# Attention scores from two float32r parts in 64-row halves of TensorE, in place of three bfloat16 parts in 96 rows

## The reference

```python
x = x + attention(layernorm(x), ctx)      # 16 heads of 16 columns
x = x + ffn(layernorm(x))                 # every operand rounded to FP4 in blocks of 16
# attention
Q, K, V = heads(x @ Wq), heads(ctx @ Wk), heads(ctx @ Wv)
attn = softmax(Q @ K.T * 16 ** -0.5)      # over all 1601 context rows
out  = heads_back(attn @ V) @ Wo + bo
# ffn
h = silu(fp4(x) @ fp4(w_gate).T) * (fp4(x) @ fp4(w_up).T)
y = fp4(h) @ fp4(w_down).T                # 704 hidden columns
```

## Time and profile before

| what | us |
|---|---|
| median of 3 runs | 3928.88 |
| fastest and slowest of them | 3926.39, 3929.58 |
| span of the profiled execution, first to last instruction | 3925.2 |
| the median less that span | 3.7 |
| TensorE (PE) busy | 3745.4 |
| VectorE (DVE) busy | 2997.8 |
| ScalarE (ACT) busy | 2260.4 |
| GpSimd (POOL) busy | 870.2 |

### The profile page before, as it was taken

One profiled execution on the slowest core, in us unless ns is written; L12 is line 12 of the kernel. 1 busy time (PEld: TensorE's weight loads), 2 busy tenths in 40 slices (PEclk: granted clock), 3 DMA queues, 4 the chain that ended last, 5 costly groups with the idle time before them and its releaser, 6 DMA issues.

```text
span 3925.2 us, 73982 instructions
## 1 busy us (share of the span) xinstructions
PE 3745.4 (95%) x19654; PEld 1618.5 (41%) x19654; DVE 2997.8 (76%) x6641; ACT 2260.4 (58%) x4414; POOL 870.2 (22%) x917
## 2 busy tenths in 40 slices
PE   7999999999999999999999999999999999999997
PEld 2324444344443444434444344443434434344434
DVE  6787787787877877777877777877788777878774
ACT  2656565555655556555565556656565565655562
POOL 2221212222112211222212122221222111222113
PEclk8999999999999999999999999999999999999998
DMA  2222121121211122121121211212111211211100
GB/s 64 50 48 54 22 57 34 33 51 34 50 33 42 39 42 49 26 48 36 39 55 23 53 34 34 53 34 47 36 39 41 43 46 29 45 38 39 37 22 7
DMA packets 148169, 157.83 MB, mean 40 GB/s; under 512 B 58129, under 2 KB 118818, under 8 KB 147746
## 3 DMA queue, kind: packets, MB, share of 16 engines
q1 hardware_dynamic: 147746, 152.78, 17.8%
HBM read 39.53 MB, written 8.39 MB: 12 GB/s over the span
## 4 chain that ended last, share of the span: by engine, by line
PE 78%; DVE 11%; issue 4%; ACT 4%; SPq 1%; DMA 1%; DVEq 0%; POOL 0%; ACTq 0%
PE out_ps L815 17%; PE score_ps L804 16%; PE piece_ps L829 16%; PE work L769 8%; PE work L780 5%; DVE piece_max L1096 4%; PE work L744 3%; ACT probs L913 3%; PE work L737 3%; PE work L743 2%; PE work L735 2%; PE work L722 1%; PE work L759 1%; PE work L753 1%; PE work L727 1%
## 5 line engine op out<-in xcount | busy, mean ns | idle before, releaser
L1096 DVE TENSOR_REDUCE piece_max<-piece_ps 128x1 f32<-128x400 f32 (+1 forms) x4096 | 2144.8, 568 | 680.1 <-PE piece_ps L829 665.2
L913 ACT ACTIVATE probs<-score_ps 128x512 f32<-128x512 f32 (+1 forms) x3328 | 1876.8, 597 | 1085.1 <-PE score_ps L804 1061.0
L829 PE MATMUL piece_ps<-k_stack,q_stack 96*128 96x400 bf16 (+1 forms) x4096 | 1294.0, 339 | 55.5 <-DVE piece_max L1096 51.1
L804 PE MATMUL score_ps<-q_stack,k_stack 99*128 99x512 bf16 (+1 forms) x3328 | 1269.1, 388 | 67.6 <-issue 20.9
L815 PE MATMUL out_ps<-probs,v_ones 128*17 128x512 f32 x6656 | 886.9, 605 | 2.1 <-ACT probs L913 0.9
L804 PEld LDWEIGHTS score_ps<-q_stack,k_stack 99*128 99x128 bf16 (+1 forms) x3328 | 326.1, 99 | 910.1 <-ACT probs L913 639.0
L829 PEld LDWEIGHTS piece_ps<-k_stack,q_stack 96*128 96x128 bf16 x4096 | 389.7, 98 | 700.5 <-DVE piece_max L1096 484.4
L1148 POOL TENSOR_TENSOR h<-h,h_grid 128x704 f32<-128x704 f32 (+1 forms) x68 | 111.2, 1636 | 1106.5 <-DVE h_grid L965 1106.5
L769 PE MATMUL work<-wgu_T,xq_T 128*128 128x256 f32 (+1 forms) x1440 | 345.8, 362 | 0.4 <-ACT xq_T L887 0.4
L769 PEld LDWEIGHTS work<-wgu_T,xq_T 128*128 128x128 f32 x1440 | 258.7, 189 | 49.0 <-ACT xq_T L887 3.4
L815 PEld LDWEIGHTS out_ps<-probs,v_ones 128*17 128x17 f32 x6656 | 110.6, 95 | 277.5 <-issue 233.3
(11 more groups left out here) (142 smaller groups left out, 2846.0 us busy)
## 6 DMA issues: line engine op xcount, KB each, us to landing
k_stack<-k_parts SPq DMA_DIRECT2D x1536, 50.0 KB, 2.2
q_stack<-q_parts SPq DMA_DIRECT2D x1536, 16.0 KB, 1.8
ctx_in<-in_ctx SPq DMA_DIRECT2D x48, 384.0 KB, 3.4
x_in<-in_x SPq DMA_DIRECT2D x16, 512.0 KB, 3.7
resid<-in_x SPq DMA_DIRECT2D x16, 512.0 KB, 3.7
out<-y SPq DMA_DIRECT2D x64, 128.0 KB, 1.9
q_stack<-neg_rows SPq DMA_DIRECT2D x192, 4.0 KB, 1.7
ctx_in<-in_ctx SPq DMA_DIRECT2D x16, 48.8 KB
```

What stands on the lines that cost most here:

```text
L804: pe.matmul(score_ps[0:r, n % SCORE_RING, :], k_stack[:, par, slot(g, j), m * P:m * P + r], q_stack[:, par, slot(g, j), :], start=True, st ...
L829: pe.matmul(piece_ps[:, n % PIECE_RING, 0:hi - lo], q_stack[0:SROWS, par, slot(g, j), t * P:(t + 1) * P], k_stack[0:SROWS, par, slot(g, j) ...
L913: act.activation(probs[0:r, step % 2, j, :], score_ps[0:r, (PER_GROUP * m + j) % SCORE_RING, :], ACT.Exp, scale=SCORE_SCALE).then_inc(prob ...
L1096: dve.tensor_reduce(piece_max[:, row, c:c + 1], piece_ps[:, n % PIECE_RING, 0:piece_at[c + 1] - piece_at[c]], AX_X, ALU.max).then_inc(piec ...
```

## The change

- Q and K are split into two parts in float32r (a float32 value rounded to fewer bits) for three in bfloat16. The products (0,0), (0,1), (1,0) are stacked: 3 x 16 = 48 rows a head, and two rows for the maxima: 50.
- A head so fits in 64 rows. `place` puts neighbouring heads of a group in the lower (partitions 0 to 63) and upper half (64 to 127); which heads are lower changes from group to group. The matmuls of `scores` and `piece` take operands from one half alone; in the built program they are placed on 64 of TensorE's 128 rows, at row 0 or at row 64, where they were placed on all 128 before.
- The split is shorter: ScalarE copies the bank of `work` out, which frees it, and GpSimd makes both parts. VectorE's subtraction (`rest`) is gone.
- `max_parts` has three operations for five. The transposed maxima are float32, and go out in four DMAs of two rows for three of one row each.
- The stacking DMAs are half as many, with twice the bytes each.
- Pieces are 400, 400, 400 and 402 columns wide (even widths; one column is computed twice).
- To make room, the output goes out from `x1` itself (`y` is gone), `xq_grid` lies in `h_grid`, `ones_row` in `heads_T`. The rows of ones in `k_stack` are written by four large memsets at the start.

```diff
-STACK = [(0, 0), (0, 1), (0, 2), (1, 0), (1, 1), (2, 0)]
+STACK = [(0, 0), (0, 1), (1, 0)]
 SROWS = len(STACK) * HEAD_DIM
-SHIFT = 3
+SHIFT = 2
+HALF = P // 2
+PAIRS = PER_GROUP + 1
...
-    piece_at = [NK * c // PIECES for c in range(PIECES + 1)]
+    PIECE_W = NK // PIECES // 2 * 2
+    piece_at = [(PIECE_W * c, PIECE_W * (c + 1)) for c in range(PIECES - 1)] + [(NK - (NK - PIECE_W * (PIECES - 1) + 1) // 2 * 2, NK)]
...
+    def place(g, j):
+
+        half = j % 2 if g % 2 == 0 else 1 - j % 2
+        pair = PAIRS - 1 if j == 0 and g >= 2 else g % 2 * 2 + j // 2
+        return half, pair
...
-        k_stack = sb("k_stack", [SROWS + SHIFT, 2, PER_GROUP + 1, KW], BF16)
-        q_stack = sb("q_stack", [SROWS + SHIFT, 2, PER_GROUP + 1, NQ], BF16)
-        k_parts = sb("k_parts", [P, 2, 3, KW], BF16)
+        k_stack = sb("k_stack", [P, PAIRS, KW], F32R)
+        q_stack = sb("q_stack", [P, PAIRS, NQ], F32R)
+        k_parts = sb("k_parts", [P, 2, 2, KW], F32)
...
                     for n, (qp, kp) in enumerate(STACK):
-                        to = slice(n * HEAD_DIM, (n + 1) * HEAD_DIM)
-                        sp.dma_start(q_stack[to, par, slot(g, j), :], q_parts[rows, half, qp, :]).then_inc(q_stacked[par][j], 16)
+                        to = slice(row_half * HALF + n * HEAD_DIM, row_half * HALF + (n + 1) * HEAD_DIM)
+                        sp.dma_start(q_stack[to, pair, :].bitcast(F32), q_parts[rows, half, qp, :]).then_inc(q_stacked[par][j], 16)
...
-                pe.matmul(score_ps[0:r, n % SCORE_RING, :], k_stack[:, par, slot(g, j), m * P:m * P + r],
-                          q_stack[:, par, slot(g, j), :], start=True, stop=True).then_inc(scores_ready, 1)
+                half, pair = place(g, j)
+                rows = slice(half * HALF, half * HALF + SROWS + SHIFT)
+                pe.matmul(score_ps[0:r, n % SCORE_RING, :], k_stack[rows, pair, m * P:m * P + r],
+                          q_stack[rows, pair, :], start=True, stop=True).then_inc(scores_ready, 1)
...
-                pe.matmul(piece_ps[:, n % PIECE_RING, 0:hi - lo], q_stack[0:SROWS, par, slot(g, j), t * P:(t + 1) * P],
-                          k_stack[0:SROWS, par, slot(g, j), lo:hi], start=True, stop=True).then_inc(pieces_ready, 1)
+                half, pair = place(g, j)
+                rows = slice(half * HALF, half * HALF + SROWS)
+                pe.matmul(piece_ps[:, n % PIECE_RING, 0:hi - lo], q_stack[rows, pair, t * P:(t + 1) * P],
+                          k_stack[rows, pair, lo:hi], start=True, stop=True).then_inc(pieces_ready, 1)
...
                 elif name == "q_proj":
-                    act.copy(q_parts[:, event[1], 0, :], work[:]).then_inc(part0_ready, 1)
+                    act.copy(q_parts[:, event[1], 1, :], work[:]).then_inc(this_drained, 1)
...
                     dve.wait_ge(shift_step, step(1))
-                    dve.tensor_copy(neg_parts[:, 0, :], neg_max[:]).then_inc(shift_step, 1)
+                    by_head = neg_max[:].rearrange("p (j t) -> p j t", j=PER_GROUP)
+                    dve.tensor_copy(neg_parts[:, 0:PER_GROUP, 0, :].bitcast(F32R), by_head).then_inc(shift_step, 1)
                     dve.wait_ge(shift_step, step(2))
-                    dve.tensor_tensor(neg_rest[:], neg_max[:], neg_parts[:, 0, :], ALU.subtract).then_inc(shift_step, 1)
-                    dve.wait_ge(shift_step, step(3))
-                    dve.tensor_copy(neg_parts[:, 1, :], neg_rest[:]).then_inc(shift_step, 1)
-                    dve.wait_ge(shift_step, step(4))
-                    dve.tensor_tensor(neg_parts[:, 2, :], neg_rest[:], neg_parts[:, 1, :], ALU.subtract).then_inc(shift_step, 1)
+                    dve.tensor_tensor(neg_parts[:, 0:PER_GROUP, 1, :].bitcast(F32R), by_head, neg_parts[:, 0:PER_GROUP, 0, :], ALU.subtract).then_inc(shift_step, 1)
...
-                    pool.tensor_tensor(parts[:, half, 1, a:a + w], rest[:, n % 2, 0:w], zero[:].broadcast_to([P, w]), ALU.add).then_inc(split_step, 1)
+                    pool.tensor_tensor(parts[:, half, 0, a:a + w].bitcast(F32R), parts[:, half, 1, a:a + w],
+                                       zero[:].broadcast_to([P, w]), ALU.add).then_inc(split_step, 1)
                     pool.wait_ge(split_step, count(nxt, 4 * (CHUNKS + 1), 2 * n + 1))
-                    pool.tensor_tensor(parts[:, half, 2, a:a + w], rest[:, n % 2, 0:w], parts[:, half, 1, a:a + w],
-                                       ALU.subtract).then_inc(split_step, 1)
+                    pool.tensor_tensor(parts[:, half, 1, a:a + w].bitcast(F32R), parts[:, half, 1, a:a + w],
+                                       parts[:, half, 0, a:a + w], ALU.subtract).then_inc(split_step, 1)
```

More of the change, by code:

```diff
@@ L24 @@
 F32 = mybir.dt.float32
-BF16 = mybir.dt.bfloat16
+F32R = mybir.dt.float32r
 I32 = mybir.dt.int32
@@ L481, in build @@
         shift_loaded = [sem(f"shift_loaded{i}") for i in range(2)]
-        y_free = [sem(f"y_free{i}") for i in range(2)]
+        x1_free = [sem(f"x1_free{i}") for i in range(2)]
         KSTACKED = 16 * len(STACK)
@@ L614, in handle @@
                     half, first = g // 2, g % 2 * PER_GROUP
+                    row_half, pair = place(g, j)
+                    if kind == "start" and j == 0:
+                        sp.wait_ge(ones_ready, 2 * (g + 1))
                     if j == 0 and g % 2 == 0:
@@ L705, in fill @@
                     pe.wait_ge(o_loaded, 2 * 16)
-                    pe.wait_ge(const_ready, 7)
-                    last = pe.matmul(work[:, 0:D], ones_row[:], bias_row, start=True, stop=True)
+                    pe.wait_ge(const_ready, 5)
+                    last = pe.matmul(work[:, 0:D], ones_row, bias_row, start=True, stop=True)
                 elif name == "x_T":
@@ L746, in fill @@
                     g = event[1]
-                    pe.wait_ge(shift_step, count(nxt if g == 0 else batch, 5 * PHASES, 5 * (g + 1)))
-                    last = pe.transpose(work[:, 0:P // 2].bitcast(BF16), neg_parts[:].rearrange("p s r -> p (s r)"), ident16[:])
+                    pe.wait_ge(shift_step, count(nxt if g == 0 else batch, 3 * PHASES, 3 * (g + 1)))
+                    last = pe.transpose(work[:, 0:P], neg_parts[:].rearrange("p j n t -> p (j n t)"), ident[:])
                 elif name == "heads_out":
@@ L992, in handle @@
                     last.then_inc(ln1_step, 1)
-                elif name in ("q_proj", "k_proj"):
-                    half = event[1]
-                    if name == "q_proj":
-                        n, a, w, parts = split_number(kind, event), 0, NQ, q_parts
-                    else:
-                        n, (a, w), parts = split_number(kind, event), chunk(event[2]), k_parts
-                    dve.wait_ge(part0_ready, count(nxt, 2 * (CHUNKS + 1), n + 1))
-                    if not (kind == "start" and n < 2):
-                        dve.wait_ge(split_step, count(nxt, 4 * (CHUNKS + 1), 2 * n - 2))
-                    dve.tensor_tensor(rest[:, n % 2, 0:w], work[:, 0:w], parts[:, half, 0, a:a + w],
-                                      ALU.subtract).then_inc(this_drained, 1)
+                    if kind == "start":
+                        write_ones()
                 elif name == "max_parts":
@@ L1006, in handle @@
                     of = nxt if g == 0 else batch
-                    step = (lambda k: count(of, 5 * PHASES, 5 * g + k))
+                    step = (lambda k: count(of, 3 * PHASES, 3 * g + k))
                     dve.wait_ge(pieces_max, count(of, PHASES * NPIECE, NPIECE * (g + 1)))
@@ L1114, in body @@
                         handle(kind, batch, drain)
-                        if kind == "start" and drain[:2] in (("k_proj", 0), ("q_proj", 0)):
-                            write_ones(split_number(kind, drain))
                         drain = None
```

75 lines of the change are left out of this document (34 added, 41 removed).

## The result

The changed kernel takes 4593.39 us (median of 4 runs, 4519.31 to 4628.58), against 3927.64 (3923.83 to 3929.58) for the kernel before, beside it: by the medians a factor of 1.17. The ratios of this document are formed from a kernel's faster runs, within 1.5% of its fastest; here these are 4519.31 and 4562.91 us, at a mean granted clock of 0.879 and 0.868, and give 1.156, 95% interval 1.151 to 1.162, while the other two had 0.854 and 0.852. The forecast of 4186 us had the sign right and missed the size; the time lies above its range. The profiled execution is the shortest of the four, with a span of 4516.8 us, so what its trace charges to the clock is the least of the four.

What follows compares the result with a forecast made beforehand. The prediction took TensorE's rate to bound the kernel. Tiling changes and bare loads +532 us, overlap -145, waits taken up -100, VectorE and the split -30 gave +257: 4186 us, 6.5% slower, range 3950 to 4430.

Steps and rivals of the forecast that it cites:

- The step that failed: TensorE's clock: distances read at 2.4 GHz were kept; a fall to 1.2 GHz was mentioned but given no price.
- drains and rounds' own loads: TensorE switching between 128-row rounds and 64-row scores or pieces: within 34.6 us a middle batch, +532 us in all with float32r.
- A drain of 0.09 us and a bare load of 0.11: Each TensorE tiling change runs empty 0.09 us, then a 4-byte weight load lies bare for about 0.11 us.
- float32r at one column a cycle, and its weights at float32's price: Scores and pieces on TensorE: one column streamed per cycle, not two; weight load 0.11 us, not 0.01.
- The rival with two cycles: float32r scores and pieces stream at two cycles a column, adding 1395 us: some 5350 us; chance 0.09.
- both with a cheap load: float32r weights load in 0.01 us: 3866 us with full overlap (chance 0.14), 3996 us with little overlap (0.04).
- Overlap in part: Neighbouring scores and pieces in opposite halves partly run at once: 8.7 us a batch, about -145 us; main case's chance 0.56.
- No overlap: Rival: scores and pieces in opposite halves never run at once: 4331 us, to 4460 without waits taken up; chance 0.17.
- Waits taken up: Drains falling where TensorE already waits for VectorE or ScalarE cost nothing: -100 us taken, between 0 and 180.
- VectorE and the split: 134 us of VectorE operations go and the bank of `work` comes free earlier: -30 us taken.
- No cost taken: GpSimd's two operations, stacking DMAs (2.2 us to landing), start memsets and output from `x1` stay hidden: nothing added.
- What the profile would show: Right if opposite halves start under 0.15 us apart, rounds lose 0.20 us either side, weight loads near 184 ns.

Runs made afterwards that it cites:

- halves_bf16_fixed: Changed kernel with scores and pieces reading one fixed bfloat16 tile instead of the stacks, same halves and rows, real scores left out: 4108.39 us, ratio 1.046.
- lower_fixed: Changed kernel with scores and pieces reading one fixed float32r tile, always in the lower half, real scores left out: 5132.99 us, ratio 1.305.
- halves_fixed: Control: changed kernel with scores and pieces reading one fixed float32r tile instead of the stacks, same halves and rows, real scores left out: 4616.55 us, ratio 1.176.
- rows128_bf16_fixed: Changed kernel with scores and pieces reading one fixed bfloat16 tile on all 128 rows, real scores left out: 3872.4 us, ratio 0.986.
- by_group_rows64: Changed kernel with each whole group in one half, the next in the other, and scores over 64 rows for 50 (zeros added): 4125.75 us, ratio 1.050.
- rows128_fixed: Changed kernel with scores and pieces reading one fixed float32r tile on all 128 rows, real scores left out: 4072.71 us, ratio 1.037.

## Why the prediction was wrong, point by point

**The step that failed** is the clock, a term put at nothing without a reason. The prediction's last sentence is: "if halves count as less activity and it fell to 1.2 GHz, all of it would be wrong". It was seen, and it got no price, no rival and no part of the range; the sum took every distance from stretches at 2.4 GHz. About half the rows in 7424 matmuls, and float32r in them, took the mean clock from 0.983 to 0.879, and that cost 18 us in each middle batch of the shortest execution; the others, at 0.852 to 0.868, are 44 to 109 us longer. That the terms at full clock add up to nearly what was taken (251 us for 257) doesn't save the forecast: they are less than half of the 592.

**The terms for a middle batch**, in us, the first four at full clock. "Taken" is the forecast's: 34.6 less float32r's 13.2 is 21.4, and where it gave a whole, a sixteenth.

| term | taken | measured | from |
|---|---|---|---|
| drains and rounds' own loads, less overlap and waits taken up | 21.4 - 8.7 - 6.3 = +6.4 | +4.5 | halves_bf16_fixed less before, 1.6, and the 2.9 below |
| of these, overlap | -8.7 | -8.5 | lower_fixed less halves_fixed, 39 steps x 4/3 |
| float32r | +13.2 | +14.1 | halves_fixed less halves_bf16_fixed |
| VectorE, split, DMAs | -1.9 | -2.9 | rows128_bf16_fixed less before |
| clock | 0 | +18.0 | after less before |

- *A drain of 0.09 us and a bare load of 0.11*: right, both read off the timeline.
- *float32r at one column a cycle, and its weights at float32's price*: right in kind. That the size fits too (14.1 for 13.2) is partly luck: on 128 rows about half of float32r's cost is a stream longer by 0.013 to 0.017 us a matmul (last section), which the forecast put at nothing, and only the rest is bare loads. The rival with two cycles and both with a cheap load are out.
- *Overlap in part*: right in kind and size (though 16 x 8.7 is 139 us and not the 145 of the sum, and the measured number carries 39 steps over to 52). With bfloat16 it is 188.6 - 184.3 = 4.3 us in the 39 steps, less than float32r's 6.4, since there is no slow load to hide.
- *No overlap* (4331 to 4460): the nearest rival by time, and wrong as a mechanism.
- *Waits taken up*: no run takes this term alone. It is right only inside the first line.
- *VectorE and the split*: somewhat larger than taken; which part gives it is open.
- *No cost taken* for the DMAs: `k_stack`'s now take 3.0 us to landing for 2.2, and PE's waits for them stay short: 4.6 us once for `k_stack`, and 7.3 us for the maxima's for 6.7 before.
- *What the profile would show*: the signs of the "right" list are there (the load records, near 184 ns in the list, are 211 and 200 over both clocks); the clock wasn't in that list.

The 14 middle batches make 14 x 33.8 = 473 us of the 592 by which the profiled spans differ. The rest lies in the start (98.8 us for 85.4), the first batch (263.3 for 220.5) and the last (345.8 for 282.8), which together spend 370 us at 1.2 GHz for 72.

## What to carry to other kernels

When a change leaves TensorE's rows idle, ask first what the granted clock does with it: keep the time of each matmul apart from the clock at which it runs, and give the second one a price and a chance. The cheap test is to pad the contraction with rows of zeros; if that makes a kernel faster, as it did here with the time at full clock unchanged, it was held by the clock. No kernel with halves came down to the kernel before: by_group_rows64, the best of those that keep the result, takes 4125.75 us. Each change of tiling costs 0.09 us, and a 4-byte operand another 0.11, so before halving count the matmuls on all rows that stand between, and the neighbours that will really overlap.

## What the hardware showed that I had not expected

- The clock falls with TensorE 97 to 98% busy in the records. It follows the rows that work: 66 rows gave 0.930, 128 rows 0.980 or above, at the same time for each matmul; 50 and 48 rows in tiles of 64, without overlap, gave 0.771. Rows of zeros count. How the chip weighs this isn't settled here.
- float32r streams a little slower than bfloat16 on the same rows. In stretches without waits, a piece to the next matmul takes 0.184 us for 0.169, and a score to a piece 0.233 for 0.216. These are medians at full clock in rows128_fixed and rows128_bf16_fixed, where score or piece stands ahead and behind, of the distances under 0.21 and 0.26 us; the means are 0.183 for 0.171 and 0.233 for 0.218. On 7424 matmuls that is an estimated 100 to 120 us of the 200 that float32r costs there. The rest fits bare loads behind `out_ps`, where a score to the next piece takes 0.337 for 0.226. First rows128_fixed, then rows128_bf16_fixed:

```profile
2101.84 0.63 PE L839 MATMUL piece_ps<-fixed 128*128 128x400 f32 x2
2102.30 0.40 PE L810 MATMUL score_ps<-fixed 128*128 128x512 f32 x1
2102.54 0.36 PE L839 MATMUL piece_ps<-fixed 128*128 128x402 f32 x1
2102.73 1.03 PE L773 MATMUL work<-wgu_T,xq_T 128*128 128x256 f32 x4
```

```profile
2106.03 0.33 PE L839 MATMUL piece_ps<-fixed 128*128 128x400 bf16 x1
2106.20 0.38 PE L810 MATMUL score_ps<-fixed 128*128 128x512 bf16 x1
2106.41 0.33 PE L839 MATMUL piece_ps<-fixed 128*128 128x402 bf16 x1
2106.58 0.38 PE L810 MATMUL score_ps<-fixed 128*128 128x512 bf16 x1
```

In float32r two pieces behind `out_ps` take 0.46 us (2101.84 to 2102.30), 0.11 of it the bare load; the score takes 0.24 and the next piece 0.19. In bfloat16 these two are 0.21 and 0.17.
